# Moving the decay and weight-staging set-up three pipeline steps later in the LayerNorm prologue of a fused recurrent/FFN kernel

## The reference

```
xn = layernorm(x)                                   # x: 4 x 4096 x 1024
decay = 0.9 + sigmoid(decay_param) * 0.099
q, k, v = xn @ Wq, xn @ Wk, xn @ Wv                 # 64 columns each
g = sigmoid(xn @ Wg + bg)                           # one gate per token
S_t = decay * S_{t-1} + (k_t g_t) outer (v_t g_t)   # scan over 4096 tokens
s = (q_t @ S_t) @ Wo + bo
h = silu(xn @ w_gate.T / 127) * (xn @ w_up.T / 127) # hidden 3072, int32 weights
out = x + s * silu(h @ w_down.T / 127)
```

## Time and profile before

| | us |
|---|---|
| median of 2 runs | 773.1 (771.13 and 775.08) |
| the profiled execution | 774.08 |
| its span, slowest core (core 2) | 772.5 |
| spans of the 8 cores | 760.5 to 772.5 |
| TensorE busy with matmuls, core 2 | 574.8 (74%) |
| VectorE busy | 221.9 (29%) |
| ScalarE busy | 128.5 (17%) |
| POOL busy | 76.8 (10%) |

### The profile page before, as it was taken

One profiled execution on the slowest core, in us unless ns is written; L12 is line 12 of the kernel. 1 busy time (PEld: TensorE's weight loads), 2 busy tenths in 40 slices (PEclk: granted clock), 3 DMA queues, 4 the chain that ended last, 5 costly groups with the idle time before them and its releaser, 6 DMA issues.

```text
span 772.5 us, 7974 instructions; the slowest of 8 cores (760.5 to 772.5 us)
## 1 busy us (share of the span) xinstructions
PE 574.8 (74%) x2740; PEld 264.3 (34%) x2740; DVE 221.9 (29%) x508; ACT 128.5 (17%) x216; POOL 76.8 (10%) x146
## 2 busy tenths in 40 slices
PE   0002354715562788888999999989999999999997
PEld 0001122312231334433444334334444444444443
DVE  1424234523534133533221222221212212122222
ACT  1102131413413020210111010011111111101010
POOL 3101121101120000100111000001111111000000
PEclk9998688759796898999999999999999999999999
DMA  8886688886796312324353223225544555203332
GB/s 184 175 153 133 136 156 189 162 120 167 133 181 131 69 28 28 55 28 54 55 81 56 84 81 109 81 83 79 83 67 74 81 82 78 32 10 100 109 110 81
DMA packets 60584, 75.36 MB, mean 98 GB/s; under 512 B 36545, under 2 KB 36673, under 8 KB 60546
## 3 DMA queue, kind: packets, MB, share of 16 engines
q0 software_dynamic: 21632, 48.24, 34.4%
q1 hardware_dynamic: 38400, 25.17, 14.0%
q10 hardware_dynamic: 514, 1.45, 0.8%
HBM read 89.53 MB, written 8.39 MB: 127 GB/s over the span
## 4 chain that ended last, share of the span: by engine, by line
PE 64%; DMA 22%; DVE 8%; issue 3%; ACT 1%; POOL 1%; DVEq 0%; SPq 0%; ACTq 0%; POOLq 0%
PE pb L709 37%; PE pb L780 22%; DMA xts<-xttm 10%; DMA xn<-xhb 7%; DMA wd_bf<-xhb 4%; PE pb L475 2%; DVE stc L317 2%; DVE xhb L347 2%; DMA abig<-wob 1%; PE pb L796 1%; DVE stc L315 1%; ACT abig L814 1%; DVE h_bf L736 1%; PE pb L508 1%; PE pb L583 0%
## 5 line engine op out<-in xcount | busy, mean ns | idle before, releaser
L709 PE MATMUL pb<-xn,gubf 128*128 128x512 bf16 x1536 | 353.6, 392 | 91.8 <-SPq L374 65.0
L709 PEld LDWEIGHTS pb<-xn,gubf 128*128 128x128 bf16 x1536 | 152.5, 101 | 282.3 <-issue 117.9
L780 PE MATMUL pb<-wd_bf,h_bf 128*128 128x512 bf16 x768 | 169.8, 379 | 8.8 <-ACT abig L814 5.9
L736 DVE SCALAR_TENSOR_TENSOR h_bf<-pb,sgbf 128x512 bf16<-128x512 f32 x96 | 66.4, 692 | 248.9 <-PE pb L709 246.9
L780 PEld LDWEIGHTS pb<-wd_bf,h_bf 128*128 128x128 bf16 x768 | 74.4, 98 | 101.6 <-issue 12.9
L731 ACT ACTIVATE sgbf<-pb 128x512 bf16<-128x512 f32 x96 | 57.0, 595 | 307.4 <-PE pb L709 307.4
L676 POOL DMA_DIRECT2D gubf<-wgu x96 | 51.1, 538 | 433.4 <-PE pb L709 354.6
L823 DVE TENSOR_TENSOR abig<-abig,pb 128x512 f32<-128x512 f32 x32 | 22.0, 688 | 138.4 <-DMA xtmt<-xttm 78.0
L317 DVE BATCH_NORM_STATS2 stc<-xts 128x6 f32<-128x512 f32 x48 | 30.1, 682 | 96.6 <-DMA xts<-xttm 96.6
L393 PE MATMUL pb<-wkvg_bf,wd_bf 128*128 128x129 bf16 x128 | 12.7, 277 | 50.1 <-SPq L374 50.1
L814 ACT ACTIVATE abig<-pb 128x512 f32<-128x512 f32 x32 | 19.2, 599 | 167.1 <-PE pb L780 167.1
(11 more groups left out here) (77 smaller groups left out, 131.8 us busy)
## 6 DMA issues: line engine op xcount, KB each, us to landing
gubf<-wgu POOLq DMA_DIRECT2D x96, 256.0 KB, 5.0
xts<-xttm POOLq DMA_DIRECT2D x16, 1024.0 KB, 7.9
xtmt<-xttm SPq DMA_DIRECT2D x16, 512.0 KB, 4.8
out<-xtmt SPq DMA_DIRECT2D x16, 512.0 KB, 3.3
wd_bf<-wdt POOLq DMA_DIRECT2D x24, 256.0 KB, 9.6
abig<-wqk ACTq DMA_DIRECT2D x1, 512.0 KB
xtmt<-wkvg ACTq DMA_DIRECT2D x1, 512.0 KB
abig<-wob ACTq DMA_DIRECT2D x1, 260.0 KB
```

What stands on the lines that cost most here:

```text
L709: e.matmul(out=o, lhsT=gu_bf[gpar][:, gu * 1024 + dc * 128: gu * 1024 + (dc + 1) * 128], rhs=xn[:, dc * N + half * 1024 + nh * 512: dc * N ...
L736: e.scalar_tensor_tensor(out=h_bf[:, hc * 1024 + nh * 512: hc * 1024 + nh * 512 + 512], in0=a, scalar=QS, in1=sg_bf[:, sgp * 512:(sgp + 1) ...
L780: e.matmul(out=o[:, dh * 512:(dh + 1) * 512], lhsT=h_bf[:, hc * 1024 + nc2 * 128: hc * 1024 + (nc2 + 1) * 128], rhs=wd_bf[:, hc * 1024 + d ...
```

## The change

In the loop that fills `pre`, decay_pre is placed ahead of step k = 5 instead of k = 2, and stage_pre ahead of k = 6 instead of k = 3. Nothing else is edited.

```diff
         for k in range(20):
-            if k == 2:
+            if k == 5:
                 pre.append(decay_pre)
                 pretag.append(("DY", 0))
-            if k == 3:
+            if k == 6:
                 pre.append(stage_pre)
                 pretag.append(("SG", 0))
             pre.append(lambda k=k: ln_bcde(k))
```

## The result

The change makes the kernel a little slower. Its median is 777.85 us over 35 runs, against 774.85 over 34 runs of the kernel before; the ratio is 1.0035 with a 95% interval of 1.0018 to 1.0052. All ratios leave out the executions in which the cores of one die ran slower at a lower granted clock. The forecast was -1.7 us, or 771.4, with a range up to 776.0: wrong in sign, and the range missed by 2 us.

The account below looks back on a forecast made before the run. The last of 32 transposes plus a constant 517 us was taken as the bound, the x loads setting that moment. Terms -4.4 + 0.4 + 0.3 + 1.3 + 0.8 = -1.6, taken as -1.7 from 773.1: 771.4 us, range 766.5 to 776.

Parts of the forecast that it names:

- the 256 at which the forecast was to fall: Failure sign: the first query/key projection (L475) on the slowest core starting before 250 or after 256 us.
- Part 1: stage_pre leaves k=3: statistics of pair 2 start at 38.0 us, not 42.38, a gain of 4.4 us (ends -8 and 0).
- X(3): Load of x pair 3: issued at 43.9 us, it takes 9.6 us instead of 9.19 in a busier queue, +0.4.
- Part 2: decay_pre at k=5, 4.13 us on VectorE under 3.8 us of cover, delays the statistics of pair 4: +0.3 us.
- the high end of 2.7 us: decay_pre's exposure at k=5 if pair 1's first transpose is delayed and TensorE's first slice starts only 1.4 us earlier.
- B(4) later than 69: Sign that decay_pre's term is wrong: the statistics of pair 4 on VectorE starting after 69 us.
- Part 3: stage_pre at k=6, ending at 86.7 us: +1.3 for wob's load traffic and +0.8 for transposes meeting loads.
- B(5): Statistics of pair 5 on VectorE, behind stage_pre: to start at 84 to 87 us, no earlier than before.
- the gate: The x load of pair 6 still waits for TensorE's second slice, not VectorE, and is issued at 93.4, not 95.86.
- D(4): Pair 4's transposes start at 91.7 us among gate and x loads; the x load of pair 6 loses 0.8 us.
- wob's bytes: wob's 0.26 MB, now loaded beside the transposes of pair 3, delay TensorE's second slice: +1.3 us (ends 0 and 3).
- Rival 2: Slower: stage_pre becomes the gate of pair 6's x load, after decay_pre lies bare for 2.7 us; 775.4 us, chance 0.15.

Follow-up runs that it names:

- e8: Kernel before with VectorE waiting for wob and casting it only behind the last LayerNorm step, second measurement: ratio 0.9952 to the kernel before.
- e5: Against the kernel before: stage_pre at k=6, decay_pre still at k=2, wob cast behind the last LayerNorm step; ratio 0.9955.
- e3: The whole change, but VectorE waits for wob and casts it only behind the last LayerNorm step; ratio 1.0027 to the kernel before.
- e2: Half of the change against the kernel before: stage_pre at k=6, decay_pre still at k=2; ratio 0.9990.
- e7: stage_pre at k=6, decay_pre at k=2, plus two awaited MEMSETs on VectorE ahead of the statistics of pair 4; ratio 1.0057 to the kernel before.
- e15: decay_pre at k=2, stage_pre with its wob wait behind the statistics of pair 5 and normalisation of pair 4; ratio 0.9937 to the kernel before.
- e9: decay_pre at k=5 but behind the normalisation of pair 3, stage_pre at k=6, wob cast late; ratio 0.9965 to the kernel before.
- e14: Kernel before with wob cast late and its load issued inside the existing step of k=17; ratio 0.9950 to the kernel before.
- e11: The change itself, measured a second time against the kernel before: ratio 1.0070, interval 1.0044 to 1.0095.

## Why the prediction was wrong

- **What bounds the kernel, right.** 517 us behind the last transpose in either kernel, and the first part decides. The first L475 of core 2 started at 261.2 for 253.4 forecast, beyond the 256 at which the forecast was to fall.
- **Part 1, the first term right.** B(2) starts at 39.05 on core 2, 37.4 as a mean, for 38.0; the wait was worth 3.7 us by e8, for 4.4.
- **Part 1, X(3), mis-sized.** I had taken 9.6 us for it, as D(0)'s transpose was still under way. From issue to B(3) it took 51.80 - 44.59 = 7.2. X(4) so went out 5.9 us early on core 2, not 4.1. This looked like more gain and became the loss of part 2.
- **Part 2, the step that failed first.** "So B(4) comes 4.13 - 3.8 = 0.3 us late". The 3.8 us of cover were the distance from v_h[0] to the landing of X(4), and I moved both ends forward by the same 4 us. They don't hang on the same thing: the landing hangs on the x loads and came 5.6 us earlier (65.7 for 71.3), v_h[0] hangs on D(1)'s transposes and came 2.2 earlier (65.39 for 67.62). That leaves 0.3 us of the cover on core 2, and on the other seven cores X(4) had landed 1.0 to 3.4 us before v_h[0] was done, so decay_pre lay bare for 3.3 us and for its whole 3.6 to 4.0 us. I had seen the case, as the high end of 2.7 us, and put it into the rivals. My sign for it, B(4) later than 69 on core 2, didn't show it (68.96), as X(4) was earlier than forecast too. By e5 against e3 decay_pre's place costs 5.6 us, by e2 against the change 3.5 to 6.2, each give or take 3 to 4, for 0.3 in the sum.
- **The rule of the Trainium skill on table loads.** In the changed kernel the Ln load at 65.52 is followed by its ACTIVATE at 66.81, 1.29 us as before (rows below). The drain that the Trainium skill gives in "ScalarE: Activation LUTs", section "What ACT_TABLE_LOAD costs", isn't seen here either, and e7 has the loss without any further table load. The rule pointed at the right place for another reason. ScalarE's timeline, core 2:

```profile
63.22 1.28 ACT L196 ACT_TABLE_LOAD   x1
64.51 0.20 ACT L196 ACTIVATE sig_s<-dec_s 1x1 f32<-1x1 f32 x1
65.52 1.28 ACT L203 ACT_TABLE_LOAD   x1 [0.80 <-DVE dcy_s L199]
66.81 0.20 ACT L203 ACTIVATE ld_s<-dcy_s 1x1 f32<-1x1 f32 x1
```

- **Part 3, B(5) and the gate right, D(4) wrong.** stage_pre ended at 86.9 on core 2 for 86.7 forecast. X(6) still waited for slice 1, but went out at 96.35, not at 93.4: C(3) ended 1.3 us later than forecast, and D(3)'s two transposes, 6.15 and 6.04 us before, took 5.92 and 8.35. And "X(6) shares the queue with a transpose and loses about 0.8 us" was far too little. I had priced a transpose among loads at 6.15 us, from a row in which one x load and two wd loads stood around it. D(4)'s second transpose met gate loads, an x load and two wd loads together, and SyncE waited up to 15.6 us for it; kvg_pair(0) came 8.6 us late on core 0 and not 3, and 8.2 as a mean. By e15 against e2 this costs 4.1 us, by e5 against e2 2.7.
- **wob's bytes, too dear.** The sum had 1.3 us for them beside D(3). From X(5)'s issue to slice 1 the means over the cores are 13.0 and 12.1 us in e5 and e9, which load wob there, against 12.3 and 12.1 in e8 and e14, which don't; the ratios of the four lie between 0.9950 and 0.9965. That leaves 0 to 0.9 us, and e14 against e8 shows none beside X(2) either.
- **The sum, with what was measured.** Terms that don't use the change's own time: -3.7 for the wait at k=3 (e8), +2.7 to +4.1 for the wait at k=6 (e2 against e5 and e15), +5.6 for decay_pre (e3 against e5), together +4.6 to +6.0. Measured were +2.7 (1.0035) and +5.4 (1.0070). The first term is uncertain by 1.9 us and the others by 3.6 or so each, the sum by some 6, so this agreement is weak support; the firmer one is that e2 is level with before and e7, e11 and the change are slower. What the wait cost at k=3 it costs at k=6 again, and decay_pre's place is the difference.
- **The rivals.** Rival 2 had the right sign and nearly the price (775.4) and one of its two causes, decay_pre bare in front of B(4). Its mechanism, stage_pre as the gate of X(6), isn't what happened: POOL's releaser for the gate loads ahead of X(6) stayed TensorE. I gave it 0.15.

## What to carry to other kernels

A cover is a distance between two events; before it is carried over to a changed schedule, each of the two must be followed by its own chain, and a gain in one of them is a loss of cover. A wait on an in-order engine costs by what stands queued behind it: 7.2 us of waiting for wob in front of a LayerNorm pair cost some 3 to 4 us, 4.5 us behind it nothing that could be measured. Where steps of a list are woven with others by count, adding or dropping a step anywhere shifts all that follow, so such a place is worth trying by itself and must be kept still in an experiment on something else.

## What the runs showed that I had not expected

- A DMA transpose of a 128 x 1024 tile, for which SyncE waited 1.8 us when nothing else moved, was waited for up to 15.6 us when gate, x and wd loads were issued just ahead of it or beside it (core 0).
- An empty step in the weaving list was worth 1.2% (0.9879), 1.7 to 3.5 times the effect of the change in question (1.0070 and 1.0035) and of the other sign.
- Without the empty step TensorE idled for 6.21 us on core 2, and the slice behind that took 2 us more than others, at a granted clock of 0.54.
